# Causal masks added by VectorE, values projected for two head groups at once, and a three-slot ring of products, in the sparse layer's attention

## The reference, cut to what matters

```python
def attention(h, wq, wk, wv, wo):            # NH = 32 heads, NKV = 8, D = 64
    b, s, _ = h.shape
    q = (h @ wq).reshape(b, s, NH, D).transpose(0, 2, 1, 3)
    k = (h @ wk).reshape(b, s, NKV, D).transpose(0, 2, 1, 3)
    v = (h @ wv).reshape(b, s, NKV, D).transpose(0, 2, 1, 3)
    k = jnp.repeat(k, GROUPS, axis=1)
    v = jnp.repeat(v, GROUPS, axis=1)
    scores = jnp.einsum('bhqd,bhkd->bhqk', q, k) / jnp.sqrt(jnp.float32(D))
    causal = jnp.tril(jnp.ones((s, s), bool))
    scores = jnp.where(causal, scores, jnp.finfo(scores.dtype).min)
    attn = jax.nn.softmax(scores, axis=-1)
    out = jnp.einsum('bhqk,bhkd->bhqd', attn, v)
    return out.transpose(0, 2, 1, 3).reshape(b, s, NH * D) @ wo
...
    h = x + attention(rmsnorm(x, ln1_w), wq, wk, wv, wo)
    return h + moe(rmsnorm(h, ln2_w), gate_w, w1, w2, w3)
```

## Time and profile before

| | |
|---|---|
| time, median of 3 runs | 2548.9 us (2547.44 to 2551.47) |
| time of the profiled execution | 2549.37 us |
| its span | 2548.1 us |
| PE busy over the span | 2059.2 us (81%) |
| DVE, ACT, POOL busy | 1544.0, 1086.2, 1074.3 us |
| mean granted share of PE's clock | 0.873 |
| steps 0 to 63 of the stage | 382.88 to 731.58 us of the span |

### The profile page before, as it was taken

The page is one execution under the profiler, slowest core; times in us unless marked ns, Lnnn a source line. Parts: engine busy times, 40 slices in busy tenths (PEclk is TensorE's granted clock), DMA queues, the critical chain, the costliest instruction groups (busy, mean ns, idle before and its releaser), DMA issues. The chain is left out here.

```text
span 2548.1 us, 35316 instructions
## 1 busy us (share of the span) xinstructions
PE 2059.2 (81%) x12705; PEld 1435.2 (56%) x12752; DVE 1544.0 (61%) x2880; ACT 1086.2 (43%) x2193; POOL 1074.3 (42%) x1101
## 2 busy tenths in 40 slices
PE   5666759999984999967546888878999988798777
PEld 2333346666763999943414454545777765555445
DVE  6877755554445777756785555544556555456546
ACT  3245626455432445535171354442444434432433
POOL 2766717556546767746543233321233222231000
PEclk8766679999986999978768888889999989989788
DMA  4222210000004565521001000020000000012000
GB/s 145 68 60 60 59 42 20 12 24 12 9 1 157 181 188 184 177 79 56 31 19 39 3 3 3 3 83 26 1 1 1 1 1 2 29 48 106 2 1 17
DMA packets 49868, 124.52 MB, mean 49 GB/s; under 512 B 5632, under 2 KB 18432, under 8 KB 47520
## 3 DMA queue, kind: packets, MB, share of 16 engines
q1 hardware_dynamic: 48160, 118.07, 14.5%
q0 software_dynamic: 1536, 4.20, 0.5%
HBM read 105.07 MB, written 16.12 MB: 48 GB/s over the span
## 5 line engine op out<-in xcount | busy, mean ns | idle before, releaser
L1837 POOL TENSOR_SCALAR l0f_probs<-l0f_probs,l0f_tot 128x128 f32<-128x128 f32 (+1 forms) x256 | 201.8, 807 | 141.7 <-DVE l0f_tot L1784 141.1
L3191 POOL TENSOR_TENSOR l2x_probs<-l2x_probs,l2x_rc 128x512 f32<-128x512 f32 x64 | 66.5, 1040 | 254.9 <-DVE l2x_rc L3092 254.9
L1306 DVE TENSOR_REDUCE l2a_a_max<-ps 128x6 f32<-128x768 f32 x128 | 119.5, 954 | 88.0 <-PE ps L1158 87.4
L1362 POOL TENSOR_SCALAR_AFFINE_SELECT l2a_a_probs<-l2a_a_probs 128x256 f32<-128x256 f32 (+1 forms) x192 | 88.3, 484 | 172.5 <-ACT l2a_a_probs L1268 148.7
L2054 PE MATMUL ps<-l0f_xh,l0f_wh 128*128 128x256 f32 x480 | 146.3, 305 | 0.1
L2171 POOL TENSOR_TENSOR l0f_wl<-l0f_raw,l0f_wh 128x1024 fp32r<-128x1024 f32 x60 | 142.0, 2386 | 0.0
L1708 ACT ACTIVATE l0f_probs<-ps,l0f_neg 128x128 f32<-128x128 f32 (+1 forms) x256 | 104.3, 424 | 87.1 <-DVE l0f_neg L1774 87.1
L2056 PE MATMUL ps<-l0f_xh,l0f_wl 128*128 128x256 f32 x480 | 136.5, 284 | 0.0
L2055 PE MATMUL ps<-l0f_xl,l0f_wh 128*128 128x256 f32 x480 | 136.5, 284 | 0.0
L3032 ACT ACTIVATE l2x_probs<-ps,l2x_neg,l2x_rs 128x256 f32<-128x256 f32 x128 | 71.0, 559 | 145.5 <-DVE l2x_neg L3082 145.4
L700 DVE TENSOR_TENSOR_SCAN l1x_h<-l1x_dA,l1x_dBu 128x512 f32<-128x512 f32 x64 | 116.6, 1860 | 8.6 <-issue 8.6
(11 more groups left out here) (722 smaller groups left out, 5828.0 us busy)
## 6 DMA issues: line engine op xcount, KB each, us to landing
l0f_raw<-in_e_l0f SPq DMA_DIRECT2D x60, 512.0 KB, 4.1
l0x_bc<-scratch_bc SPq DMA_DIRECT2D x32, 512.0 KB, 4.8
l0f_raw_d<-in_e_l0f SPq DMA_DIRECT2D x60, 256.0 KB, 3.0
scratch_rows<-zero SPq DMA_DIRECT2D x1, 3840.0 KB, 18.9
l0f_xb<-scratch_rows SPq DMA_DIRECT2D x15, 256.0 KB, 3.1
scratch_results<-l0f_yb SPq DMA_DIRECT2D x15, 256.0 KB, 2.3
l0f_slab<-in_g_l0f SPq DMA_DIRECT2D x8, 448.0 KB, 3.5
l2f_ew<-in_e_l2f SPq DMA_DIRECT2D x8, 384.0 KB, 3.0
```

What stands on the lines that cost most here:

```text
L1306: dve.tensor_reduce(M[:, 2 * half:2 * half + 2, j, :], src.rearrange("p a (c n) -> p a c n", c=NB_), AX.X, ALU.max).then_inc(*unit_max.tick())
L1362: last = pool.affine_select(part, part, [[0, m], [1, P]], ALU.is_ge, 0.0, base=0, channel_multiplier=-1)
L1837: last = pool.tensor_scalar(pr[:, u % 3, a, r], pr[:, u % 3, a, r], tot[:, u % 3, qt, a:a + 1], None, ALU.mult)
```

## The change

1. The four mask matmuls of `score` are gone. DVE adds the mask (`self.mask`, float32, in SBUF) to both diagonal blocks of both banks in one `tensor_tensor` of 128 x 512 elements, PSUM in and PSUM out, before its two maxima, and waits for its own result between.
2. v is projected for two groups at a time, in two halves of four token tiles (i = 6 and 7), in the last two steps ahead of an even group only; there 8 matmuls of 128 columns stand in each half. Ahead of an odd group there is no v. `vt` holds two groups a slot, ACT still copies 128 x 512 elements a half.
3. O of a sequence comes as soon as its two units are weighed: in step u + 5 for every odd unit u, so in even steps only (8g + 6, 8g + 8, 8g + 10, 8g + 12). `oT` shrinks from two whole groups to a ring of three sequences. The last step is 68, it was 74.
4. The slab of an even group has 1024 columns, that of an odd one 768.

```diff
     def a_of(n):
         g, i = n // 8 + 1, n % 8
-        return [(g, i)] if i < 7 and g < NG else []
+        return [(g, i)] if g < NG and (i < 6 or g % 2 == 0) else []
...
     def o_of(n):
-        g, i = (n - 11) // 8, (n - 11) % 8
-        return [(g, i)] if i < 4 and 0 <= g < NG else []
-
-    STEPS = range(-8, N + 11)
+        u = n - 5
+        return [(u // 8, u % 8 // 2)] if u % 2 and 0 <= u < N else []
+
+    STEPS = range(-8, N + 5)
...
-                    w = slab[:, g % 2, 768:896].rearrange("p (c n) -> p c n", c=2)
-                    for t in range(NT):
+                    w, t0 = slab[:, 0, 768:1024].rearrange("p (c n) -> p c n", c=2), 4 * (i - 6)
+                    for t in range(4):
                         for c in range(2):
-                            last = pe.matmul(bank[:, t * hd:(t + 1) * hd], xT[:, c, t * P:(t + 1) * P], w[:, c, :], start=c == 0, stop=c == 1)
+                            last = pe.matmul(bank[:, t * P:(t + 1) * P], xT[:, c, (t0 + t) * P:(t0 + t + 1) * P], w[:, c, :], start=c == 0, stop=c == 1)
...
-                    pe.matmul(bank[:, P:P + S], qT[r, z, p, t0 + P:t0 + S], kT[r, z, t0:t0 + S], start=False, stop=False)
-                for i, (unit, mask) in enumerate(((k.identb, k.mask_qk), (k.ident_swap, k.mask_swap))):
-                    for r, bank in halves:
-                        diagonal = bank[:, 0:512].rearrange("p (q n) -> p q n", n=S)[:, :, 0:P]
-                        last = pe.matmul(diagonal, unit[r, :], mask[r, :].unsqueeze(1).to_broadcast([64, 2, P]), start=False, stop=i == 1)
+                    last = pe.matmul(bank[:, P:P + S], qT[r, z, p, t0 + P:t0 + S], kT[r, z, t0:t0 + S], start=False, stop=True)
...
-                    pe.wait_ge(*taken(8 * g + 8))
+                pe.wait_ge(*taken(8 * g + 2 * i + 2))
...
-                if u % 8 == 0 and g >= 2:
-                    act.wait_ge(*out_ps(4 * (g - 1)))
-                act.copy(oT[:, g % 2, p, b * S:(b + 1) * S], ring("V", u, 0)[:, 0:S]).then_inc(*taken.tick())
+                if p == 0 and u >= 6:
+                    act.wait_ge(*out_ps(u // 2 - 2))
+                act.copy(oT[:, u // 2 % 3, p, :], ring("V", u, 0)[:, 0:S]).then_inc(*taken.tick())
...
                 banks, m = ps[:, 2 * (u % 2):2 * (u % 2) + 2, :], neg[:, u % 3, :, :]
+                diagonal = banks.rearrange("p a (q n) -> p a q n", n=S)[:, :, :, 0:P]
+                dve.tensor_tensor(diagonal, diagonal, k.mask.unsqueeze(1).unsqueeze(1).to_broadcast([P, 2, 2, P]), ALU.add).then_inc(*vc.tick())
+                dve.wait_ge(*vc.now())
                 dve.tensor_reduce(m[:, 0, :], banks[:, :, 0:P], AX.X, ALU.max).then_inc(*vc.tick())
```

More of the change, by code:

```diff
@@ L138, in pack_inputs @@
             np.tile(g[f + "wk"].reshape(2, P, 8, 1, 64), (1, 1, 1, 2, 1)).transpose(2, 1, 0, 3, 4).reshape(8, P, 256),
-            g[f + "wv"].reshape(2, P, 8, 64).transpose(2, 1, 0, 3).reshape(8, P, 128),
+            np.repeat(g[f + "wv"].reshape(2, P, 4, 128).transpose(2, 1, 0, 3).reshape(4, P, 256), 2, 0),
             g[f + "wo"].reshape(8, 2, P, 256).transpose(0, 2, 1, 3).reshape(8, P, 512)], 2)),
@@ L202, in __init__ @@
         self.mask_qk = self.kb[:, 128:256]
+        self.mask = self.kf[:, 368:496]
         self.mask_kq = self.kb[:, 256:384]
@@ L1566, in a_of, with nth, all_of @@
         g, i = n // 8 + 1, n % 8
-        return [(g, i)] if i < 7 and g < NG else []
+        return [(g, i)] if g < NG and (i < 6 or g % 2 == 0) else []
+    def nth(g, i):
+        return 7 * g + g % 2 + i + 1
+    def all_of(g):
+        return nth(g, 5 if g % 2 else 7)
     def o_of(n):
-        g, i = (n - 11) // 8, (n - 11) % 8
-        return [(g, i)] if i < 4 and 0 <= g < NG else []
-    STEPS = range(-8, N + 11)
+        u = n - 5
+        return [(u // 8, u % 8 // 2)] if u % 2 and 0 <= u < N else []
+    STEPS = range(-8, N + 5)
     uses, place = [], {}
@@ L1593, in ring_free @@
             return added(4 * a + i + 1)
-        if i == 6:
-            return v_sb(a + 1)
+        if i >= 6:
+            return v_sb(a + i - 5)
         return k_sb(2 * a + i // 3 + 1) if i % 3 == 2 else q_sb(4 * a + i // 3 * 2 + i % 3 + 1)
@@ L1599, in l0f_attention @@
         sb = k.buffers(cx, "l0f_")
-        slab, out_w = sb("slab", [P, 2, 896]), sb("out_w", [P, 2, 512])
+        slab, out_w = sb("slab", [P, 2, 1024]), sb("out_w", [P, 2, 512])
         wh, wl = sb("slab_h", [P, 2, 768], F32R), sb("slab_l", [P, 2, 768], F32R)
         xh, xl = sb("xTh", [P, 2, TOK], F32R), sb("xTl", [P, 2, TOK], F32R)
-        qT, kT, vt = sb("qT", [P, 2, 2, TOK]), sb("kT", [P, 2, TOK]), sb("v", [P, 2, NT, hd])
-        oT, pr, pT = sb("oT", [P, 2, 2, TOK]), sb("probs", [P, 3, 2, 384]), sb("probsT", [P, 2, 2, 384])
+        qT, kT, vt = sb("qT", [P, 2, 2, TOK]), sb("kT", [P, 2, TOK]), sb("v", [P, 2, NT, 2 * hd])
+        oT, pr, pT = sb("oT", [P, 3, 2, S]), sb("probs", [P, 3, 2, 384]), sb("probsT", [P, 2, 2, 384])
         scan.prepare(cx)
@@ L1665, in weigh @@
                 pe.wait_ge(*t_dve(u + 1))
-                pe.wait_ge(*v_sb(g + 1))
+                pe.wait_ge(*v_sb(2 * (g // 2) + 2))
                 pe.wait_ge(*ring_free("V", u, 0))
@@ L1669, in weigh @@
                     for a in range(2):
-                        last = pe.matmul(bank[64 * a:64 * a + 64, kt * P:S], vt[:, g % 2, 2 * b + kt, :], pT[:, u % 2, a, kt * S:kt * S + S - kt * P],
+                        last = pe.matmul(bank[64 * a:64 * a + 64, kt * P:S], vt[:, g // 2 % 2, 2 * b + kt, g % 2 * hd:(g % 2 + 1) * hd], pT[:, u % 2, a, kt * S:kt * S + S - kt * P],
                                          start=kt == 0, stop=kt == 1, tile_position=(0, 64 * a))
@@ L1681, in project_back @@
                     for c in range(2):
-                        last = pe.matmul(bank[:, t * D:(t + 1) * D], oT[:, g % 2, c, (2 * i + t) * P:(2 * i + t + 1) * P], out_w[:, g % 2, c * D:(c + 1) * D],
+                        last = pe.matmul(bank[:, t * D:(t + 1) * D], oT[:, (4 * g + i) % 3, c, t * P:(t + 1) * P], out_w[:, g % 2, c * D:(c + 1) * D],
                                          start=c == 0, stop=c == 1)
@@ L1712, in take @@
             def take(g, i):
-                act.wait_ge(*proj(7 * g + i + 1))
+                act.wait_ge(*proj(nth(g, i)))
                 bank = ring("A", g, i)
@@ L1719, in take @@
                 else:
-                    if g >= 2:
-                        act.wait_ge(*product(8 * (g - 1)))
-                    act.copy(vt[:, g % 2].rearrange("p t d -> p (t d)"), bank).then_inc(*v_sb.tick())
+                    if g >= 4:
+                        act.wait_ge(*product(8 * (g - 2)))
+                    act.copy(vt[:, g // 2 % 2, 4 * (i - 6):4 * (i - 5), :].rearrange("p t d -> p (t d)"), bank).then_inc(*v_sb.tick())
             def take_turned(u):
@@ L1739, in high @@
                 if g >= 2:
-                    act.wait_ge(*proj(7 * (g - 1)))
+                    act.wait_ge(*proj(all_of(g - 2)))
                 act.copy(wh[:, g % 2, :], slab[:, g % 2, 0:768]).then_inc(*w_hi.tick())
@@ L1748, in at_act @@
                 for g, i in a_of(n):
-                    if i % 3 != 2 or i == 6:
+                    if i % 3 != 2:
                         take(g, i)
@@ L1776, in take_k @@
             def take_k(g, i):
-                dve.wait_ge(*proj(7 * g + i + 1))
+                dve.wait_ge(*proj(nth(g, i)))
                 if g >= 2:
@@ L1842, in load_slab @@
                 if g >= 2:
-                    sp.wait_ge(*proj(7 * (g - 1)))
+                    sp.wait_ge(*proj(all_of(g - 2)))
                     sp.wait_ge(*w_lo(g - 1))
-                sp.dma_start(slab[:, g % 2, :], k.dram["g_l0f"][g, :, 0:896]).then_inc(*slab_in[g % 2].tick())
+                n = 768 if g % 2 else 1024
+                sp.dma_start(slab[:, g % 2, 0:n], k.dram["g_l0f"][g, :, 0:n]).then_inc(*slab_in[g % 2].tick())
             load_slab(0)
@@ L1852, in at_sp @@
                     sp.wait_ge(*out_ps(4 * (g - 1)))
-                sp.dma_start(out_w[:, g % 2, :], k.dram["g_l0f"][g, :, 896:1408]).then_inc(*out_in[g % 2].tick())
+                sp.dma_start(out_w[:, g % 2, :], k.dram["g_l0f"][g, :, 1024:1536]).then_inc(*out_in[g % 2].tick())
             for s in (slab_in[0](4), slab_in[1](4), out_in[0](4), out_in[1](4)):
```

## The result

The changed kernel took 2572.6 us (median of 4 runs, 2570.3 to 2573.9), the kernel before 2550.2 beside it (2547.4 to 2555.3): ratio 1.0085, 95% interval 1.0066 to 1.0103. I had forecast 2549, within 2536 to 2561, and had put 0.30 on slower.

A forecast was written before the change was run, and what follows sets the result against it. PE was taken to bound the stage, busy 330.5 of 348.7 us. Sum: -33.3 work, +1.9 O, waits 21.2 to 44.8, -1.6, -2.7, +0.3 = -11.8; +12.0 clock = +0.2, so 2549 us, range 2536 to 2561.

The forecast's parts named there:

- position 6: Step of each group where `turn` waits for POOL: 3.64 us, or 1.69 ahead of even groups; 16.0 in all.
- position 0: Step of a group behind one without v: `turn` waits 1.39 us, twice, 2.8 in all.
- position 3: Step of a group where A waits for `take_out` to free a bank: 1.0 us each in groups 1, 5, 6.
- the even steps from 56 on: Last eight steps, without A: each even step waits 2.9 us, four times, 11.6 in all.
- DVE's price: DVE's added mask instruction per unit: 0.69 us plus 0.03 for its own wait; each 0.1 us moves the total 2.1.
- the write to PSUM costs more: Rival, between score and maxima: DVE's add takes longer than 0.69 us; at 1.2 us the kernel takes 2560; chance 0.16.
- PE stays the bound: Rival for the stage: waits do not grow and the whole 33 us less PE work shows, 2516 us; chance 0.07.
- PE's clock: Long waits in the stage halve PE's clock: 8 falls at 1.5 us, +12.0, less 1.6 for an old one.
- falls at every wait from 1.4 on, or for longer: Rival on PE's clock in the stage: 8 further falls, +12 us, 2561 us; chance 0.14.
- The term for idle: PE's waits in the stage: 44.8 us after the change against 21.2 before.
- my tail: Work from the wait of `turn`(62) to the last O: 13.5 us instead of 16.2, saving 2.7; that wait 3.7.
- What leaves PE: PE work removed in the stage: masks 19.9 us and values 13.4, together 33.3.

The follow-up runs named there:

- k_late: The changed kernel with DVE's k copy moved behind the maxima and `invert` of its step; 2543.0 us, ratio 0.9963 to the kernel before.
- inv_first: The changed kernel with `invert(n - 1)` as DVE's first instruction of a step, ahead of k copy, mask add and maxima; 2548.2 us, ratio 0.9979 to the kernel before.
- inv_k: The changed kernel with DVE's order set to `invert(n - 1)`, then mask add and maxima, then k copy; 2528.6 us, ratio 0.9902 to the kernel before.
- act_mask_new: inv_k with ACT's copy of the turned block moved ahead of the exponentials; 2514.2 us, ratio 0.9843 to the kernel before.
- values_only: The kernel before with only v projected for two groups at once and the matching slab sizes; 2542.5 us, ratio 0.9951 to the kernel before.

## Why the prediction was wrong

**Right: the places and the causes.** `turn` waits at position 6 in rows (each about 0.16 short of the real stretch, as in the prediction) of 3.93, 4.26 and 3.51 us (ahead of odd groups; forecast 3.64) and 2.28, 1.54 and 1.53 (ahead of even ones; forecast 1.69), at position 0 twice (2.01 and 1.94; forecast 1.39); A at position 3 waits for `l0f_oT` 0.81, 0.81 and 1.46 (forecast 1.0) and in step 35 4.12 (4.3); the even steps from 56 on wait 2.75 or 2.76 (2.9). DVE's price, which I had called the lever, was right to 0.01. The rival that the write to PSUM costs more is refuted by its row, "PE stays the bound" by the waits.

**Wrong: three sizes, all on the same side.** The stage came out at +22.3 where the sum says +0.2. The 22.1 between them:

- *The step "PE's clock": 8 falls at 1.5 us, 12.0, less the old one, +10.4 net.* Measured 19.9: PE's busy time fell by 8.7 where its work at full clock fell by 28.6 (below), so 9.5 short. The clock's records say the same: 46.6 us of PE's busy time lay at 1.2 GHz, 6.8 before, and half of the difference is 19.9. They have 10 falls in the stage, 6 of them of 6.8 us and 4 of 3.4, where the stage before has two, both of 3.4. One costs 5.74 - 3.53 = 2.2 at step 38, where it begins 2.1 us ahead of `turn`, and 6.49 - 3.53 = 3.0 in the tail, where it begins 0.6 ahead: about half of the busy time that it covers. I had priced all by the one case that the earlier trace rows show, with 1.57. This is the largest miss. The rival "falls at every wait from 1.4 on, or for longer" (2561, 0.14) had its second half right and its first wrong: the waits of 1.54, 1.94, 2.01 and 2.28 brought none.
- *The term for idle: in the sum it stands at +23.1 for the stage.* Measured 52.6 - 21.6 = +31.0, 7.9 short. No single wait was far off: with the 0.16 added back, position 6 came out longer by 2.0 in all, position 0 by 1.5, position 3 by 1.4; an early step had 1.2 where I had nothing, the scan's steps 0.6 more, and `turn`(62) 0.6 more than my tail had. In step 38 a part is visible: from POOL's start to `turn` it is 610.54 - 606.74 = 3.80 us, where the earlier trace rows have 3.03. The second of POOL's four instructions took 1.68 us beside DVE's instruction on 1024 elements at 607.00, the fourth, of the same size, 0.92.
- *"What leaves PE", 33.3 us.* Measured 28.6, in starts of PE's work kind by kind: the masks gave 0.22 a unit, 13.8 in 64, not 19.9, because score now takes 0.85 from start to start (626.74 to 627.59, say) instead of 0.76. The values gave 14.0 (seven groups of 3.62 before, six halves of 1.89 after; I had 13.4), and 0.8 came from small differences elsewhere.

9.5 + 7.9 + 4.7 = 22.1. The line between the first two is not sharp: the fall in the old tail, about 1.6, stood in the sum inside the -2.7, and the 0.3 of the slab lies ahead of step 0. Booked with the clock, the 1.6 makes the misses 11.1 and 6.3, and the clock's stays the largest. The range was too narrow because I treated these as independent sizes with two far ends each, though the long waits and the clock belong to the same places.

**What my sum did not ask.** I read "as latency it lies in front of the maxima, so of the exponentials, of `invert`, of POOL" as a fact of the algorithm. It was one of the order on DVE: `invert` needs nothing of the add, and k_late, inv_first and inv_k show that some 44 us hang on two moves of a few lines. No rival of mine had it, because all of them took the queue as given.

Still open: why a fall lasts 3.4 us at one place and 6.8 at the next with the same wait and the same work (two of the four even steps of the tail each way), why waits of one length at one place are followed by a fall in one kernel and by none in another, and whether masks on PE with O in even steps gain from ACT's new order too; that kernel was not run, so how much of act_mask_new's gain needs the mask on DVE is not settled.

## What to carry to other kernels

Before work is moved to an engine that "has room", list that engine's queue for the step and ask which later engine waits for something behind the moved instruction; put the result that others wait for first (here: sums' reciprocal, maxima, copies for the next group). Edits that each remove PE work also remove each other's cover: alone these three summed to about zero in time (+9 us in the stage), together to 22 us lost. When PE's waits grow to 2 or 3 us, price the fall of the clock with them, and allow for falls longer than the ones seen so far.

## What the runs showed of the hardware

- **Falls of the clock.** At the same kind of place PE ran at 1.2 GHz for 3.4 us or for 6.8, though it was busy again from `turn` on. In the changed kernel all ten waits from 2.75 us on were followed by one and none of 2.28 and less was. That is no fixed bound: in inv_k a wait of 2.62 had none, and three of four waits of 1.91 in the last steps had (weigh 1.48 there instead of 0.80). In values_only a wait of 2.98 had none and one of 2.00 had, at the place where 1.99 had none before:

```profile
411.89 0.87 PE L1666 MATMUL ps<-kf,l0f_probs 128*128 128x128 f32 x6 [2.98 <-POOL l0f_probs L1845]
...
434.28 1.54 PE L1666 MATMUL ps<-kf,l0f_probs 128*128 128x128 f32 x6 [2.00 <-POOL l0f_probs L1845]
```

So the length of the wait does not decide alone. The Trainium skill (TensorE: Matmul & The Clock Gate, Why this matters for your kernels) asks for no PE idle gaps above about 3 us. These traces have falls after shorter ones, of 1.91, 2.00 and 2.75.
- **Leaving a half-height tile.** Score's second half takes 0.53 us to the start of a projection (627.06 to 627.59 in the changed kernel) where it took 0.44 ahead of the mask matmuls, which also use 64 rows. So the four masks were worth 0.22 and not the 0.32 between their start and the next start. The Trainium skill (TensorEngine Tiling (Array Packing), Key Properties) says that changing the tiling mode drains TensorE. The rows fit that, if the 0.1 us falls to whichever 64-row matmul is the last ahead of a full one. They do not prove it, since the mask matmuls are bf16 and no run takes them apart from their type.
- **DVE from PSUM to PSUM.** 128 x 512 float32 elements cost 0.695 us, beside 0.687 with the result in SBUF: no surcharge for the write in this case.
- **POOL beside DVE.** One POOL instruction took 1.68 us instead of 0.92 while DVE ran a `tensor_tensor` of 1.21 us with both inputs in SBUF; the four of the unit took 3.80 to `turn` instead of 3.03. The Trainium skill (GPSIMD Engine Reference, Specifications) names contention with DVE instructions that have two SBUF inputs; the row agrees.
